# Gated output biases of a four-expert layer: a matmul for each tile and expert, or sums on GpSimd

## The reference, cut to what matters

```
def _L1_ffn_ref(x, gate_w, gate_b, w1, b1, w2, b2):
    scores = jnp.einsum('bsd,de->bse', x, gate_w) + gate_b
    probs = jax.nn.softmax(scores, axis=-1)
    ...
    masked = masked / (jnp.sum(masked, axis=-1, keepdims=True) + 1e-09)
    h = jax.nn.gelu(jnp.einsum('bsd,edh->ebsh', x, w1) + b1[:, None, None, :], approximate=False)
    y = jnp.einsum('ebsh,ehd->ebsd', h, w2) + b2[:, None, None, :]
    out = jnp.einsum('bse,ebsd->bsd', masked, y)
    return out
...
t = t + _L1_attn_ref(_ln_t(t), ...)
t = t + _L1_ffn_ref(_ln_t(t), ...)
```

## Time and profile before

| what | value |
|---|---|
| median of 3 runs | 1714.9 us (1713.95 to 1715.45) |
| the profiled execution's own time | 1715.7 us |
| its span, first to last instruction | 1713.9 us |
| PE busy | 1587.9 us, 93% |
| DVE busy | 1194.9 us, 70% |
| ACT busy | 905.5 us, 53% |
| POOL busy | 172.5 us, 10% |
| mean granted TensorE clock | 0.975 of full speed |

### The profile page before, as it was taken

The page is one execution under the profiler, slowest core; times in us unless marked ns, Lnnn a source line. Parts: engine busy times, 40 slices in busy tenths (PEclk is TensorE's granted clock), DMA queues, the critical chain, the costliest instruction groups (busy, mean ns, idle before and its releaser), DMA issues.

```text
span 1713.9 us, 32585 instructions
## 1 busy us (share of the span) xinstructions
PE 1587.9 (93%) x13136; PEld 1026.2 (60%) x13136; DVE 1194.9 (70%) x2544; ACT 905.5 (53%) x1330; POOL 172.5 (10%) x247
## 2 busy tenths in 40 slices
PE   1589999999999999999999999989999999999998
PEld 0334576556665576655765567655666556655666
DVE  6766775957757677767758587586776767686643
ACT  2313655366544665456653565536654566535654
POOL 2020003001020012000030010200111000300000
PEclk9667999999999999999999999999999999999999
DMA  4221002010020101110020100201001100200000
GB/s 131 96 56 38 1 2 66 1 48 2 1 65 15 35 1 40 26 48 1 2 65 1 48 1 1 66 2 48 1 24 43 47 1 1 66 1 11 1 11 10
DMA packets 25243, 48.16 MB, mean 28 GB/s; under 512 B 7427, under 2 KB 16963, under 8 KB 23717
## 3 DMA queue, kind: packets, MB, share of 16 engines
q1 hardware_dynamic: 15840, 28.44, 6.0%
q0 software_dynamic: 6144, 9.45, 2.4%
q10 hardware_dynamic: 3110, 8.21, 1.4%
HBM read 20.70 MB, written 6.29 MB: 16 GB/s over the span
## 4 chain that ended last, share of the span: by engine, by line
PE 67%; DVE 22%; ACT 4%; issue 3%; DMA 2%; POOL 1%; SPq 0%; DVEq 0%; ACTq 0%
PE ps L426 20%; PE ps L697 16%; PE ps L644 10%; DVE mx L1118 7%; PE ps L461 6%; PE ps L585 3%; DVE acc L1277 3%; DVE room L1293 3%; PE ps L505 2%; DVE norm_stats L959 1%; PE ps L433 1%; PE ps L492 1%; PE ps L465 1%; ACT room L843 1%; DVE gn_st L1001 1%
## 5 line engine op out<-in xcount | busy, mean ns | idle before, releaser
L843 ACT ACTIVATE room<-ps,b_sb 128x512 f32<-128x512 f32 x384 | 263.3, 686 | 457.7 <-PE ps L426 457.6
L697 PE MATMUL ps<-wout_h,room 128*128 128x192 f16 x3072 | 458.6, 246 | 5.4 <-DVE acc L1277 5.4
L1293 DVE SCALAR_TENSOR_TENSOR room<-room 128x512 f16<-128x512 f32 x384 | 262.7, 687 | 178.6 <-ACT room L849 173.8
L697 PE MATMUL ps<-wout_l,room 128*128 128x192 f16 x1536 | 377.5, 246 | 0.0
L697 PEld LDWEIGHTS ps<-wout_h,room 128*128 128x128 f16 x3072 | 286.1, 98 | 45.7 <-DVE acc L1277 11.8
L825 ACT ACTIVATE room<-ps 128x1024 f32<-128x1024 f32 (+3 forms) x288 | 225.1, 811 | 161.9 <-PE ps L465 124.4
L1118 DVE TENSOR_REDUCE mx<-ps 128x2 f32<-128x1024 f32 (+3 forms) x288 | 265.8, 952 | 35.3 <-PE ps L589 20.3
L849 ACT ACTIVATE room<-room 128x512 f16<-128x512 f32 x384 | 241.8, 630 | 34.3 <-ACT room L843 0.7
L644 PE MATMUL ps<-room,v 128*64 128x512 f32 (+3 forms) x1152 | 232.5, 488 | 0.0
L585 PE MATMUL ps<-qk 96*128 96x512 f16 (+3 forms) x576 | 160.6, 350 | 38.8 <-DVE mx L1118 29.8
L697 PEld LDWEIGHTS ps<-wout_l,room 128*128 128x128 f16 x1536 | 150.2, 98 | 27.2
(11 more groups left out here) (205 smaller groups left out, 2297.2 us busy)
## 6 DMA issues: line engine op xcount, KB each, us to landing
xc<-x_ch SPq DMA_DIRECT2D x8, 768.0 KB, 5.6
qk<-qk_all SPq DMA_DIRECT2D x96, 64.0 KB, 2.4
qk<-qk_all POOLq DMA_DIRECT2D x96, 64.0 KB, 2.6
out<-acc ACTq DMA_DIRECT2D x16, 384.0 KB, 3.1
xt<-x_tok SPq DMA_DIRECT2D x7, 768.0 KB, 6.9
qk<-qk_all POOLq DMA_DIRECT2D x96, 32.0 KB, 2.0
qk<-qk_all SPq DMA_DIRECT2D x96, 32.0 KB, 2.5
room<-w_in SPq DMA_DIRECT2D x2, 1024.0 KB, 10.8
```

What stands on the lines that cost most here:

```text
L697: mm = pe.matmul(dst, hid[:, s, tok], w[:, n, :], start=(k == 0 and m == 0 and t % 2 == 0), stop=False, skip_group_check=True)
L843: act.activation(h32[:, i % N_H, :], ps[:, H_BANK[i], :], ACT.Gelu, scale=1 / (U_SCALE * W_SCALE), bias=b1_sb[:, n:n + 1])\
L1293: V.scalar_tensor_tensor(out=h_l[:, s, :], in0=h32[:, s, :], scalar=A_SCALE, in1=h_h[:, s, :], op0=ALU.mult, op1=ALU.subtract)\
```

## The change

The 256 bias matmuls are dropped, and the last matmul of an expert closes its sum. The bias is loaded into all 128 partitions as f32 (`b2_sb`, 384 KB in place of 6 KB), and GpSimd scales it once. For each block it then runs a new function, `add_gated_biases`: for each expert a product of the gate, broadcast over 192 channels, with the bias, broadcast over four tiles, into `b2_gated`, and an addition of that to `acc`. Those are eight operations of 128x768 f32 a block, each of which waits for the one before. Since VectorE also adds into `acc`, the two take turns: the sums of block 0 wait for the add of y = 1 (`BIASES_AFTER` = 2), and VectorE waits for them before y = 2; the sums of block 1 must be done before y = 4. In GpSimd's queue the sums of block 0 stand behind the gate exponential, then comes the next image's power for norm 1, then the sums of block 1, then that image's key DMAs.

```diff
@@ -66,7 +66,8 @@
 HALVES = (slice(0, P // 2), slice(P // 2, P))
 F_LAG = 3
 N_P32, N_H = 5, 4
-N_FILLS = 11
+BIASES_AFTER = 2
+N_FILLS = 8
 
 
 
@@ -168,7 +169,8 @@
         wout_l = sb("wout_l", [P, CHUNKS, C], F16)
         wo32 = sb("wo32", [P, 2, C], F32)
         b1_sb = sb("b1_sb", [P, CHUNKS], F32)
-        b2_sb = sb("b2_sb", [P, EXPERTS * C], F16)
+        b2_sb = sb("b2_sb", [P, EXPERTS, C], F32)
+        b2_gated = sb("b2_gated", [P, TB, C], F32)
         gb_sb = sb("gb_sb", [P, NT, EXPERTS], F32)
 
 
@@ -265,9 +266,6 @@
         bq_st = sb("bq_st", [CC, 2, 4], F32)
         bq_t = sb("bq_t", [CC, 4, 2], F32)
         wc = u[0:CC + 1, :, :].rearrange("p t c -> p (t c)")[:, 0:2 * NCV].rearrange("p (c n) -> p c n", c=2)
-        acc_flat = acc[:, :, :].rearrange("p t c -> p (t c)")
-        b2_st = acc_flat[0:2, 0:4 * C]
-        b2_t = acc_flat[0:2, 4 * C:6 * C].bitcast(F16)
 
         ps = ctx.enter_context(nc.psum_tensor("ps", [P, 8, QB], F32))
 
@@ -282,7 +280,9 @@
         setup_pool = sem("setup_pool")
         setup_act = sem("setup_act")
         consts_ready = sem("consts_ready")
-        b2_ready = sem("b2_ready")
+        b2_scaled = sem("b2_scaled")
+        b2_step = sem("b2_step", NB * (2 * EXPERTS - 1))
+        b2_added = sem("b2_added", NB)
 
 
         x_ch_in = sem("x_ch_in", 16)
@@ -695,12 +695,8 @@
                         for m, (hid, w) in enumerate(((h_h, wout_h), (h_h, wout_l), (h_l, wout_h))):
 
                             mm = pe.matmul(dst, hid[:, s, tok], w[:, n, :],
-                                           start=(k == 0 and m == 0 and t % 2 == 0), stop=False,
-                                           skip_group_check=True)
-                        if k == HC - 1:
-
-                            mm = pe.matmul(dst, b2_ones[:, :], b2_sb[:, e * C:(e + 1) * C],
-                                           start=False, stop=True, skip_group_check=True)
+                                           start=(k == 0 and m == 0 and t % 2 == 0),
+                                           stop=(k == HC - 1 and m == 2), skip_group_check=True)
                     mm.then_inc(f2_done, 1)
 
                 aside = Aside(tail(img, 1, True))
@@ -724,7 +720,6 @@
             first.until(FRONT_AT["turn"])
             pe.wait_ge(stage_lo, len(pieces))
             first.finish()
-            pe.wait_ge(b2_ready, 1)
             attend(0, False)
             for img in range(B - 1):
                 experts(img, Aside(front(img + 1, True)))
@@ -860,7 +855,7 @@
                 act.dma_start(bn_st[rows, :, :], bn_rows[rows]).then_inc(rows_in, 16)
             act.dma_start(bq_st[:, :, :], bn_q).then_inc(rows_in, 16)
             act.dma_start(xt[:, :, :], x_tok[0]).then_inc(x_tok_in, 16)
-            for dst, src in ((b1_sb[:, :], b1), (b2_st[:, :], b2), (gb_sb[:, :, :], gate_b),
+            for dst, src in ((b1_sb[:, :], b1), (b2_sb[:, :, :], b2), (gb_sb[:, :, :], gate_b),
                              (wo32[:, :, :], w_out[:, CHUNKS * C:].rearrange("p (k c) -> p k c", k=2))):
                 act.dma_start(dst, src).then_inc(late_in, 16)
             act.wait_ge(setup_dve, 2)
@@ -890,8 +885,7 @@
             fills = ((minus_half[:, :], -0.5), (euler[:, :, :], float(np.e)), (v32[:, :, D:2 * D], 1.0),
                      (rcp[:, :], 1.0),                     (xs[CC:CC + 1, :, :], 1.0),
                      (k4[3 * D:3 * D + 2, :, :], M_SCALE), (o32[TAIL:TAIL + 1, 1, :], A_SCALE),
-                     (b2_sb[:, :], 0.0),
-                     (b2_ones[:, :], 0.0), (wc[CC:CC + 1, :, :], 0.0), (b2_ones[0:2, :], A_SCALE))
+                     (wc[CC:CC + 1, :, :], 0.0))
             assert len(fills) == N_FILLS
             for n, (dst, value) in enumerate(fills):
                 nc.gpsimd.memset(dst, value).then_inc(setup_pool, 1)
@@ -919,11 +913,13 @@
                                 pool.dma_start(k4[dst, r:HEADS:2, tok], qk[row, k, 1:3, tok])\
                                     .then_inc(keys_in[b], 16)
 
-            def attend(img):
-
+            def norm_power(img):
                 pool.wait_ge(var_ready, at(var_ready, img, 2))
                 nc.gpsimd.tensor_tensor(norm1.pow[:, :], norm1.var[:, :], minus_half[:, 0:NT], ALU.pow)\
                   .then_inc(pow_done, 1)
+
+            def attend(img):
+
                 spread_keys(img)
 
                 def power_of_tail(b):
@@ -940,13 +936,48 @@
                 nc.gpsimd.tensor_tensor(gex[:, :, :], euler[:, :, :], gsc[:, :, :], ALU.pow)\
                   .then_inc(gate_exp, 1)
 
+            def add_gated_biases(img, b):
+
+                pool.wait_ge(tail_step, at(tail_step, img, (b + 1) * TAIL_STEPS))
+                if b == 0:
+
+                    pool.wait_ge(y_used, at(y_used, img, BIASES_AFTER))
+                tiles, done = slice(b * TB, (b + 1) * TB), b * (2 * EXPERTS - 1)
+                if img or b:
+
+                    pool.wait_ge(b2_added, at(b2_added, img, b))
+                for e in range(EXPERTS):
+                    if e:
+
+                        pool.wait_ge(b2_step, at(b2_step, img, done + 2 * e - 1))
+                    part = b2_gated[:, :, :]
+                    nc.gpsimd.tensor_tensor(part, gate[:, tiles, e:e + 1].broadcast_to([P, TB, C]),
+                                            b2_sb[:, None, e, :].broadcast_to([P, TB, C]), ALU.mult)\
+                      .then_inc(b2_step, 1)
+                    pool.wait_ge(b2_step, at(b2_step, img, done + 2 * e + 1))
+                    add = nc.gpsimd.tensor_tensor(acc[:, tiles, :], acc[:, tiles, :], part, ALU.add)
+                    if e < EXPERTS - 1:
+                        add.then_inc(b2_step, 1)
+                        pool.wait_ge(b2_step, at(b2_step, img, done + 2 * e + 2))
+                add.then_inc(b2_added, 1)
+
             group_power(0)
+            pool.wait_ge(late_in, 16 * n_late)
+            nc.gpsimd.tensor_scalar(b2_sb[:, :, :], b2_sb[:, :, :], A_SCALE * W_SCALE, None, ALU.mult)\
+              .then_inc(b2_scaled, 1)
+            pool.wait_ge(b2_scaled, 1)
+            norm_power(0)
+            attend(0)
             for img in range(B - 1):
-                attend(img)
                 group_power(img + 1)
                 gate_exp_of_block_1(img)
-            attend(B - 1)
+                add_gated_biases(img, 0)
+                norm_power(img + 1)
+                add_gated_biases(img, 1)
+                attend(img + 1)
             gate_exp_of_block_1(B - 1)
+            for b in range(NB):
+                add_gated_biases(B - 1, b)
 
 
         @block.vector
@@ -1274,6 +1305,9 @@
                         n = b * TB + t
                         if y and t == 0:
                             dve.wait_ge(y_used, at(y_used, img, y))
+                        if t == 0 and y in (BIASES_AFTER, EXPERTS):
+
+                            dve.wait_ge(b2_added, at(b2_added, img, 2 if y == EXPERTS else 1))
                         ins = V.scalar_tensor_tensor(
                             out=acc[:, n, :], in0=ps[:, 2 + t // 2, (t % 2) * C:(t % 2 + 1) * C],
                             scalar=gate[:, n, e:e + 1], in1=acc[:, n, :], op0=ALU.mult, op1=ALU.add)
@@ -1358,10 +1392,6 @@
                 first.until(PIECE_AT[n])
             first.until(FRONT_AT["maxima"] - 0.5)
             dve.wait_ge(late_in, 16 * n_late)
-            step(V.tensor_scalar(b2_t[:, :], b2_st[:, :], W_SCALE, None, ALU.mult))
-            step(V.tensor_scalar(b2_st[:, :], b2_st[:, :], W_SCALE, None, ALU.mult))
-            step(V.tensor_scalar(b2_t[:, :], b2_t[:, :], kst[0:2, K_ROW:K_ROW + 1], None, ALU.mult))
-            V.tensor_tensor(b2_sb[0:2, :], b2_st[:, :], b2_t[:, :], ALU.subtract).then_inc(b2_ready, 1)
             first.finish()
             attend(0, False)
             for img in range(B - 1):
@@ -1423,7 +1453,7 @@
         "w_in": w_in,
         "w_out": w_out.reshape(P, OUT_CHUNKS * C),
         "b1": g["L1_ffn_b1"].reshape(CHUNKS, P).T,
-        "b2": np.broadcast_to(g["L1_ffn_b2"].reshape(1, EXPERTS * C), (2, EXPERTS * C)),
+        "b2": np.broadcast_to(g["L1_ffn_b2"], (P, EXPERTS, C)),
         "gate_b": np.broadcast_to(g["L1_ffn_gate_b"], (P, NT, EXPERTS)),
     }
     arrays = {k: np.ascontiguousarray(v) for k, v in arrays.items()}
```

More of the change, by code:

```diff
@@ L258, in build @@
         gate = sb("gate", [P, NT, EXPERTS], F32)
-        b2_ones = sb("b2_ones", [P, P], F16)
         bn_st = qk_all[0:CC + 1, 0:24 * C].bitcast(F32).rearrange("p (k c) -> p k c", k=4)
```

## The result

The changed kernel takes **1887.4 us** (median of 4 runs, 1886.4 to 1888.0), 1.101 times the kernel before, 95% interval 1.0996 to 1.1023. It is slower by 172.6 us. The forecast was slower by 45 us, range 1700 to 1805.

What follows compares the result with a forecast made beforehand. TensorE was taken to bound the kernel (67% of the chain), with VectorE's late work moving the end. 1715.7 - 16.6 + 42 + 7 + 12 + 1, less 0.8, gave 1760 us; range 1700 to 1805.

Steps and rivals of the forecast that it cites:

- An operation's price: Each GpSimd operation of 128x768 f32 was estimated at 1.7 us, so 13.6 us a burst of eight.
- The key DMAs: Loads queued on GpSimd behind the second burst would move by at most 6 us, within their slack, and cost nothing.
- The matmuls' -16.6: Dropping 256 bias matmuls from TensorE saves 16.6 us, with six of eight groups on the chain in images 0 to 6.
- The last image: First burst plus VectorE's conflicting work makes 18.9 us against a window of 11.9 before y = 2: +7 us.
- the window must hold the sum of both: Before y = 2, 13.6 us of GpSimd plus 10.4 of VectorE against 18.0: 6.0 us late, seven times, +42 us.
- The second burst: After the next image's norm power, VectorE's short instructions wait out one GpSimd operation an image: +12 us, bounds 0 to 42.
- the rival of fitting bursts: No exclusion between GpSimd and VectorE, only the last image overruns by 1.7 us: 1701 us, faster; chance 0.27.
- One sum of the rivals: Without exclusion, at about 2.35 us per GpSimd operation nothing of the gain would be left.
- The evidence for exclusion: GpSimd's power of 128x8 grew by 0.37 us with an L1293 under way, read as exclusion at SBUF reads; chance 0.56.

Runs made afterwards that it cites:

- experiment 2: Kernel before, all bias matmuls kept, plus sixteen same-size GpSimd operations an image at the same places on a tile nobody reads: 1887.9 us, ratio 1.1015.
- experiment 4: Changed kernel with each GpSimd product and addition cut into two of 384 columns: 1839.2 us, ratio 1.0732.
- Experiment 6: Changed kernel with block 1's sums starting only when the next image's norm is written: 1816.3 us, ratio 1.0595.
- experiment 1: Changed kernel without GpSimd's sums and VectorE's waits for them, output bias left out: 1712.6 us, ratio 0.9992.
- experiment 5: Kernel before with bias matmuls only for y = 5 and 6 and no sums, most output bias left out: 1712.6 us, ratio 0.9989.
- experiment 8: Changed kernel, sums moved behind y = 3 and y = 7, stores one step later, last image's block 1 first after y = 1: 1712.0 us, ratio 0.9988.

## Why the prediction was wrong

**Right.** The direction, and the mechanism's kind: GpSimd and VectorE exclude each other at their SBUF reads. An operation's price (1.7 us, measured 1.75). The key DMAs: they start at 521.31, released by their own data, so the burst cost them nothing. The matmuls' -16.6: within the changed kernel, where the clock does not fall behind the short pauses, the spared intervals give about 15.

**Luck.** The last image: +7 forecast, 7.6 measured. The forecast had VectorE waiting for the end of the burst in a window too short. It did not wait; the 7.6 are a stall of 5.06 us by turns and the clock behind it, and experiment 2 loses 7.0 us there without any wait.

**The step that failed** is "the window must hold the sum of both", +42 us for the first burst. It failed in two ways. *The rule:* VectorE's small instructions were entered with their own 0.2 us. Each paid a whole GpSimd operation. Eight operations against a dense file of conflicting instructions make eight turns, 10.8 us of delay (experiments 2 and 4). *The place:* the deadline was taken to be the add of y = 2, with 18.0 us of room. VectorE works in order, and TensorE waits for the spikes behind the gate chain (L1247, L1066, then L513) long before; there the room is nil (0.05 us in before, from 440.66 to 440.71), and the delay went through one for one. The burst itself, 455.33 to 469.93, took 14.6 us and would have fitted the window of 18.0.

**The second burst** failed by the same rule, and by its count: one operation an image (+12), bounds zero and three, from L980, L982 and the copies alone. L988 was left out. It reads one SBUF tile, 192 columns in 375 ns, and there are eight of them an image, in two rows of four; the first row stands on the path that TensorE waits for. With it that path holds seven turns, and the stall grew by 10 us. Experiment 6 took this burst away from them and won 71 us.

**A term that was missing:** the clock. Each stall of 10.6 us is followed by 5 us at half speed, 2.5 us, fourteen times: 35 us of the 173 (and once more in the last image). Put together, seven images x (10.67 + 10.03 + 5.0) = 180 against the +54 forecast for the two bursts.

**The matmuls' term alone** is right by its row and worth almost nothing (experiments 1, 5 and 8): a pause of TensorE that was harmless in before is followed there by 1.2 to 1.35 us more in most images. It is not the missing matmuls that bring the clock down: with all of them kept it falls in each image but the last of experiment 2, and with none of them it does not in after. That the clock falls is shown; why it falls behind such a pause in one kernel or image and not in another stays open. So a gain of this size can be there or not by what no run here explains. So the rival of fitting bursts had the wrong time as well: with no collision at all the kernel stands at 1712, not 1701. One sum of the rivals is slightly off: by its own terms nothing of the gain is left at about 2.4 us an operation, not 2.35.

The evidence for exclusion was weighed rightly as present, and misread in size: the power of 128x8 had grown by 0.37 us, the rest of one L1293. That is a turn seen from GpSimd's side, where it costs the rest of a short instruction. Seen from VectorE's side the same turn costs the rest of a long one.

## What to carry to other kernels

Before moving work to GpSimd, list VectorE's instructions in the stretch where it will run, by what they read (two SBUF tiles, or, in a `tensor_scalar` or a copy, f32 from one), and count instructions, not their time: each can cost one whole GpSimd operation, and short dependent ones are the worst. Put GpSimd's work where VectorE waits for others or reads PSUM; here the same 128 operations cost 175 us in one place and nothing in another. If it can't be moved, cut the operations shorter: 384 columns for 768 gave back 48 us.

## What the runs showed of the hardware

- A fill of SBUF, which reads nothing, holds a f32 `tensor_scalar` (768 columns: 560 to 1544 ns; 192 columns: 375 to 1381) and leaves VectorE's instructions with two SBUF inputs untouched (686, 226 ns).
- An f32 `tensor_scalar` of four columns (L1243) waits for a GpSimd operation like any other: 1.31 us for 0.17.
- VectorE's instructions that read PSUM, with at most one SBUF tile beside it, are not held: in experiment 8 a maximum of 128x512 takes 680 ns beside a GpSimd operation and 685 away from one (L1148, medians), and an `acc` instruction of 192 columns 407 and 408 (L1309).
- A pause of TensorE of 1.1 to 1.3 us can be followed by 3 us at PEclk 0.50 or 0.52 (experiments 1 and 2), and the same pause in another kernel is not (before and after), whether the bias matmuls are there or not; a pause of 10.6 us was followed by 5 us at 0.50 in both bursts of image 1.
